# A bound on the indices of the gathers in a graph-attention kernel

## The reference

```
h_src, h_dst = x[src], x[dst]
e     = leaky_relu([h_src, h_dst, edge] @ W_attn + b_attn)
m     = [h_src, edge] @ W_ne
alpha = softmax of e over the edges with the same dst
z     = sum over those edges of alpha * m
out   = layernorm(x + relu([x, z] @ W_out))
```

## Time and profile before

| | |
|---|---|
| median of 2 runs | 4008.62 us (4007.27 to 4009.97) |
| the profiled execution | 4021.12 us, its span 4019.2 us |
| POOL busy | 2972.2 us, 74% |
| DVE busy | 2837.8 us, 71% |
| PE, weight loads, ACT busy | 56%, 50%, 50% |
| DMA engines, share of packets | 53.6% in three queues |
| granted TensorE clock, mean | 0.592 |

### The profile page before, as it was taken

One profiled execution on the slowest core, in us unless ns is written; L12 is line 12 of the kernel. 1 busy time (PEld: TensorE's weight loads), 2 busy tenths in 40 slices (PEclk: granted clock), 3 DMA queues, 4 the chain that ended last, 5 costly groups with the idle time before them and its releaser, 6 DMA issues.

```text
span 4019.2 us, 47762 instructions
## 1 busy us (share of the span) xinstructions
PE 2260.2 (56%) x9822; PEld 2005.2 (50%) x9823; DVE 2837.8 (71%) x5649; ACT 2020.9 (50%) x3433; POOL 2972.2 (74%) x3133
## 2 busy tenths in 40 slices
PE   2666655555555555555555555555555555555556
PEld 1555555544454444454444444544444544454456
DVE  8776666666766767676676766676767676766777
ACT  2665555544454444444444444444444444444446
POOL 7777777777777777777777777777777777777770
PEclk9665556556556565555655555555655556555557
DMA  6655555555555555555555555555555555555542
GB/s 166 177 173 156 159 157 156 160 158 157 158 157 157 157 157 157 157 157 157 158 157 157 157 157 157 157 158 157 157 157 157 157 157 158 157 157 157 158 147 66
DMA packets 409354, 627.14 MB, mean 156 GB/s; under 512 B 208412, under 2 KB 208796, under 8 KB 409332
## 3 DMA queue, kind: packets, MB, share of 16 engines
q1 hardware_dynamic: 296260, 519.51, 40.7%
q0 software_dynamic: 100000, 102.60, 12.3%
q10 hardware_dynamic: 13072, 4.80, 0.6%
HBM read 621.58 MB, written 4.81 MB: 156 GB/s over the span
## 4 chain that ended last, share of the span: by engine, by line
POOL 73%; issue 24%; DVE 1%; PE 1%; POOLq 1%; ACT 0%; DMA 0%; DVEq 0%
POOL V L372 73%; POOLq L390 0%; PE psE L909 0%; POOLq L381 0%; PE psT L902 0%; PE psG L844 0%; DVE y L801 0%; DVE var L782 0%; DMA V<-in_x_dram,srcs 0%; DVE y L778 0%; DVE mean L791 0%; DVE y L798 0%; DVE prod L785 0%; DMA srcs<-in_src_dram 0%; ACT zb L522 0%
## 5 line engine op out<-in xcount | busy, mean ns | idle before, releaser
L372 POOL DMA_INDIRECT V<-in_x_dram,srcs x3125 | 2971.2, 951 | 956.0 <-issue 952.9
L844 PE MATMUL psG<-V,pT 128*128 128x130 f32 x6250 | 1461.4, 427 | 366.6 <-DVE psS L663 366.6
L844 PEld LDWEIGHTS psG<-V,pT 128*128 128x128 f32 x6250 | 1361.5, 330 | 506.1 <-DVE psS L663 506.1
L837 PE MATMUL psT<-ident,e 128*128 128x128 f32 x3125 | 720.8, 404 | 1286.3 <-DVE e L658 1286.3
L448 ACT COPY pT<-psT 128x512 f32<-128x512 f32 x784 | 420.9, 589 | 1714.8 <-PE psT L837 1708.9
L837 PEld LDWEIGHTS psT<-ident,e 128*128 128x128 f32 x3125 | 573.8, 215 | 1392.7 <-DVE e L658 1392.7
L594 DVE TENSOR_TENSOR prod<-V,psM 128x512 f32<-128x512 f32 x782 | 502.4, 684 | 637.6 <-DMA V<-in_x_dram,srcs 621.8
L658 DVE TENSOR_TENSOR e<-zb,psE 128x1024 f32<-128x1024 f32 x392 | 478.8, 1221 | 259.4 <-DVE u L599 162.1
L705 DVE CUSTOM_DVE_ANT_0 um<-ubc,psS 128x1024 f32<-128x1024 f32 x391 | 477.6, 1221 | 20.2 <-ACT psS L461 19.3
L599 DVE TENSOR_REDUCE u<-prod 128x8 f32<-128x1024 f32 x391 | 477.0, 1220 | 13.5
L469 ACT ACTIVATE psE<-um,ebias 128x1024 f32<-128x1024 f32 x391 | 437.2, 1118 | 12.8
(11 more groups left out here) (97 smaller groups left out, 524.7 us busy)
## 6 DMA issues: line engine op xcount, KB each, us to landing
ubc<-scores SPq DMA_DIRECT2D x391, 512.0 KB
dbc<-in_dst_dram SPq DMA_DIRECT2D x390, 512.0 KB, 4.0
V<-in_edge_attr_dram SPq DMA_DIRECT2D x390, 256.0 KB, 2.8
V<-in_x_dram,srcs POOLq DMA_INDIRECT x3125
srcs<-in_src_dram SPq DMA_DIRECT2D x390, 4.0 KB
scores<-u SPq DMA_DIRECT2D x390, 4.0 KB
out_dram<-y SPq DMA_DIRECT2D x12, 256.0 KB
xt<-in_x_dram ACTq DMA_DIRECT2D x6, 448.0 KB, 14.2
```

The lines of the kernel that those rows point to most:

```text
L372: nc.gpsimd.indirect_dma_start(Vx[:, s, j, 1:XW], None, x[:, :], bass.IndirectOffsetOnAxis(ap=srcs[:, s, j:j + 1], axis=0)).then_inc(h_in[ ...
L837: last = nc.tensor.transpose(psT[:, i, (j - 4 * i) * P:(j - 4 * i + 1) * P], e1[:, 0:n * P].rearrange("q (p j) -> q j p", j=n)[:, j, :], i ...
L844: last = nc.tensor.matmul(psG[:, 0:AW], pT[:, i, (j - 4 * i) * P:(j - 4 * i + 1) * P], V[:, LEADIN + s * SLOT + XW * j:LEADIN + s * SLOT + ...
```

## The change

Each gather gets two more arguments: an upper bound for its indices, the number of rows of `x` less one (12,499), and the choice that an index above the bound is skipped, not reported as an error. Before, a gather had no bound, and the choice stood at its default, an error.

```diff
             def gather(s, n):
                 for j in range(n):
                     nc.gpsimd.indirect_dma_start(Vx[:, s, j, 1:XW], None, x[:, :],
-                                                 bass.IndirectOffsetOnAxis(ap=srcs[:, s, j:j + 1], axis=0)).then_inc(h_in[s], 16)
+                                                 bass.IndirectOffsetOnAxis(ap=srcs[:, s, j:j + 1], axis=0), bounds_check=x.shape[0] - 1, oob_is_err=False).then_inc(h_in[s], 16)
```

## The result

The changed kernel takes 4165.7 us (median of 2 runs, 4165.55 to 4165.85) against 4008.62: a ratio of 1.0389, 95% interval 1.0372 to 1.0407 (the two medians alone give 1.0392). It is slower by 157 us, or 157.1 / 3125 = 50.3 ns per gather. The forecast was no change.

The account below looks back on a forecast made before the run. The prediction took POOL's gathers, one after another, to bound the kernel. The register move at nothing and the check at 16 us gave 4009 + 16 = 4025 us, with a range from 3850 to 4750 us.

Parts of the forecast that it names:

- What bounds the kernel: POOL's gathers and the gaps between them hold 97% of the span; a nanosecond more per gather costs 3.1 us.
- The register move at nothing: Move ahead of each gather on POOL's sequencer, 29 ns, costed at nothing because the sequencer runs 12 gathers ahead.
- The exposed move: Rival, 4%: the sequencer loses its lead, each gather pays at least 29 ns, 4100 us.
- The check at 5 ns a gather, 16 us: Comparing each gather's 128 indices with the bound, in vectors of 16: 8 steps, 5 ns a gather, 16 us.
- the two ends worked out from the select: From POOL's select against a memset, 0.6 ns a step: 8 steps give 5 ns, 128 steps 80 ns a gather.
- The argument from the even durations: Gathers take 947 ns median, 941 minimum, whatever their indices: mostly fixed cost, so the check is a few steps.
- The check by index: Rival, 32%: indices checked one by one in the gather, 80 up to 237 ns, 4260 us, from 4090 to 4750.
- The signs: Gather medians to tell cases apart: 947 to 967 ns the forecast, 1,030 or more index by index, near 1,900 branching.
- 26 ns a gather: About 2%, 80 us: what a measurement can tell from no change; the forecast fails above it in either direction.
- The branch per index: Rival, 6%: the check branches for each index, at most doubling a gather's 947 ns, about 6,970 us.
- Shorter gathers: Rival, 15%: if reporting an error costs something now, gap or gather shrinks; 3853 us for 50 ns less.
- A change that does nothing: Case within the forecast: the bound is not looked at where no index exceeds it, 4009 us.

## Why the prediction was wrong

**What bounds the kernel** was right. Before and after, POOL's gathers followed one another without waiting for a slot or, but for the first, for a transfer, and the 158 us more of them passed into the time whole. The loss shows on DVE as longer waits for gathers, as forecast for every slower case, with its busy time at 2838.8 us.

**The register move at nothing** was right, and so was its reason. The sequencer stays 12 gathers ahead, and both a kernel with one move and one with 12,500 more sequencer instructions took the time that this gives. The exposed move, at 4100 us, is refuted.

**The check at 5 ns a gather, 16 us, was the step that failed.** It measured 50 ns, 157 us. The price lay between the two ends worked out from the select, 5 and 80 ns, and I took the lower. The mistake was in what the ends were taken to be: both were a count of steps times a cost per step, 8 or 128 of 0.6 ns. No run shows such steps. The runs show a price that hardly goes by steps at all, 44 ns at 32 rows and 39 at 64. The argument from the even durations was correct as far as it went: the body is mostly fixed per gather and has no work that depends on the data. The conclusion was not: a fixed body can get a fixed addition, and "a few steps" said nothing about its size. In hindsight, POOL's smallest whole instruction would have been the nearer row for an addition of fixed size. In POOL's groups of the kernel before it is this one (mean ns behind the comma):

```profile
L927 POOL MEMSET const-float32-0.0<- 128x1 f32 x1 | 0.1, 100 | 0.2 <-issue 0.2
```

With 100 ns as an upper end, 5 ns would have been hard to defend as the value to take. That such a row bounds an addition is not shown, and here it is twice what was measured.

**The check by index** had 4090 to 4750 us, which holds the result, but its mechanism is refuted: by index, 32 rows would have paid a quarter. That the wide range holds the result is therefore luck. The signs had a hole as well: a median up to 967 ns stood for the forecast and one from 1,030 ns on for the check by index, and 997 ns lies in neither. And 26 ns a gather was far from the least that can be told: the interval of the ratio is 7 us wide to each side, some 2 ns a gather.

**The branch per index** is refuted by its price, 50 ns where 947 were named, and by the kernel that skips half of the rows at the same 997 ns. The Trainium skill's 12 cycles per element for data-dependent branching ("GPSIMD Engine Reference", section 3.1) thus does not describe this check, whose 128 indices pay 50 ns together; the measurement decides. **Shorter gathers** are refuted by the skip without a bound, at a ratio of 1.0001. What spoke against that rival, that without a bound there is nothing to compare with, is what the runs bear out. **A change that does nothing** is refuted too: a bound of 2 to the 30th costs as much, and one of 6,249 takes half of the bytes away.

Left open is what POOL does in the 40 to 50 ns, compare or only take up the bound, and in the 13 ns more of the error: the trace has one record per gather and nothing inside it.

No kernel with a bound and 128 rows per gather came out at the time of before; where no index can exceed the table, the bound is best left away.

## What to carry to other kernels

On an engine that issues its DMAs back to back, an option of a DMA can be priced per issue: here a bound on the indices adds 50 ns to 947, and 3,125 gathers make 157 us of it, while the choice of skipping alone adds nothing. For an option that the trace does not show, think of a fixed addition per instruction beside one that goes by element. The engine's smallest whole instruction gives a first size, which in this one case was twice too high. Sequencer work is another matter, and its share in the chain does not settle it: find out first how far the sequencer is ahead, by what stands in the program before a row of the sequencer and how much of it had started by then.

## What had not been expected of the hardware

- The gather's cost hardly goes by rows: 867 ns for 32 rows, 903 for 64, 947 for 128, and 305 ns between two gathers in each case.
- The packets of the gathers' queue do not count rows: there are 100,000, or 32 for each gather, with 128, 64 and 32 rows and with half of the rows skipped. The bytes follow the rows: 102.60, 51.40, 25.80 and 52.21 MB.
- With a bound, the error is dearer than the skip, 1010 against 997 ns a gather, though no index was out of range.
- The moves make the sequencer's own pace visible at the start of the changed kernel, where it gains its lead. In the chain in order of time (start us, us, what) they come 0.54 us apart, where a gather takes 1.30:

```profile
6.30 0.03 POOLq L372
6.33 0.51 issue
6.84 0.03 POOLq L372
```
